# Recurrent attention and gated MLP layer on eight cores: fp32 transposes of the normalised input, an earlier place for the row-sum reciprocals, shorter wait lists in the down projection and at the fences

## The chip, the cores and the metric

One Trainium2 chip, eight cores, the same program on each, every core with two of the sixteen sequences; nothing passes between cores. The metric is device time in microseconds (us) of the slowest core. The engines are named as the profile names them: PE (matmuls), PEld (its weight loads), DVE (vector), ACT (scalar), POOL and SP. SP issues most DMAs; ACT's queue also issues some.

## The reference, cut to what matters

```python
xn = _layernorm(x)                         # x: 16 x 2048 x 1024, fp32
q, k, v = split_heads(xn @ Wq + bq), ...   # 16 heads of 64
att = softmax(causal(q @ k.T / 8))
y   = (att @ v) @ Wo + bo
s   = (y - mu) * rsqrt(var + eps) * gamma + beta
h   = silu(xn @ wg.T / 127) * (xn @ wu.T / 127)     # 3072 hidden, int weights
g   = silu(h @ wd.T / 127)
x   = x + s * g
```

## The kernel before, in words

Precision is kept by splitting fp32 values in two bf16 parts, "hi" (the rounded value) and "lo" (the rest), and multiplying hi by hi, hi by lo and lo by hi. All instructions are listed in program order for each engine (`W.op`), with the tokens each one waits for; an engine runs its list strictly in that order. Every compute engine has one counting semaphore (`c_te`, `c_ve`, `c_se`, `c_ge`), and a token is a value of it.

The stages, one after another with a fence between (`W.fence`, line 109: each engine puts a nop that waits for the DMAs it has issued, and everything behind the fence waits for the nops of all engines):

1. Once: weights are split or transposed and written to DRAM (lines 240 to 335).
2. For each of the two sequences, LayerNorm. A first pass reads 16 tiles of 128 tokens for the sums (lines 358 to 388). The second pass (lines 390 to 434) reads each tile again; ACT writes the normalised tile once as bf16 (`hi`, line 397) and once as fp32 (`v6`, line 402); DVE subtracts them (`lo`, line 409); PE transposes the eight 128x128 blocks of hi, and then those of lo, through one PSUM bank in bf16 (line 420), and DVE copies the bank into the arena after each eight (line 427). The bank is used again only after that copy.
3. Attention for eight head pairs (`hg`). Per pair: K and Q projections (line 551), V projection (line 603) with fp32 transposes of V (line 623), and then four query blocks (`qb`) of 512 columns. Block `qb` has `4 qb + 4` key chunks `sc`. The order of issue for each chunk is: scores of `sc` for two heads (line 736, on the diagonal also a mask matmul, line 745), exponentials of `sc` on ACT (line 760), then attention times V of chunk `sc - 1` (line 783, fp32) into banks 3 and 4, whose row 64 collects the row sums.
   The end of a block is `emit_evac` (line 660). It is called for block `qb` when scores and exponentials of chunk 0 of block `qb + 1` have been issued, and for the last block straight behind it. For each of the two heads: ACT takes Ln (line 667) and Exp with scale -1 (line 671) of the row sums, a one-row matmul spreads the reciprocals over 128 partitions into bank 5 (line 675), ACT copies bank 5 out (line 679), and DVE multiplies (line 684). The second head's matmul waits for the first head's copy, because both use bank 5. Then come the hi and lo parts (lines 694, 699) and two DMAs from ACT's queue, the second of which waits for lo.
4. Output projection (line 897) and the second LayerNorm.
5. Gated MLP for eight blocks of 256 tokens. For each of 24 hidden chunks `hc`: gate matmuls (line 1017), up matmuls (line 1029), and the chain Silu on ACT (line 1039), product on DVE (line 1045), hi on ACT (line 1054), lo on DVE (line 1059). Gate and up use banks 0 to 3 by parity. Then the down projection (line 1093) over the same 24 chunks into the same banks 0 to 3, weights coming through two buffers of two chunks each, refilled from SP's queue.

Of the kernel before, what the change touches and what calls it, by code (L numbers as in the profile page):

```python
# [57 lines left out]
class W:  # L58
    def __init__(self, nc, ctx):
        self.nc = nc  # L60
        self.ctx = ctx
        self.ops = {e: [] for e in ENG}
        self.nsem = 0
        self.barrier = []
        self.fence_sem = self.sem("fence")
        self.qsem = {e: self.sem("q_" + e) for e in ("sync", "scalar", "gpsimd")}
        self.dma_sems = {e: [self.qsem[e]] for e in ("sync", "scalar", "gpsimd")}
        self.phase_ops = {e: 0 for e in ENG}
# [38 lines left out]
    def fence(self):  # L107
        toks = []
        for e in ENG:
# [35 lines left out]
def build_program():  # L145
# [79 lines left out]
    c_ge = w.sem("c_ge")  # L225

# [109 lines left out]
    for b in range(B_PER_CORE):  # L336
# [8 lines left out]
        hi_tm = [PB[:, 16384:17408], PB[:, 17408:18432]]  # L345
        lo_tm = [PB[:, 18432:19456], PB[:, 19456:20480]]
# [3 lines left out]
        hl_cons = [[], []]  # L350
# [39 lines left out]
        for tt in range(16):  # L390
# [5 lines left out]
            hi = w.op("scalar", (lambda e, d=hi_tm[s], x_=xt[s], tt=tt:  # L396
                                 e.activation(d[:, :], x_[:, :], AF.Identity,
                                              bias=rb16[:, tt:tt + 1],
                                              scale=r16[:, tt:tt + 1])),
                      waits=[tok, s3] + hl_cons[s], inc=c_se)  # L400
# [4 lines left out]
                      waits=[tok] + xn_cons[s], inc=c_se)  # L405
            xt_cons[s] = [v6, hi]
            xn_cons[s] = []
            lo = w.op("vector", (lambda e, d=lo_tm[s], a=xnt[s], h=hi_tm[s]:
                                 e.tensor_sub(d[:, :], a[:, :], h[:, :])),
                      waits=[hi, v6] + hl_cons[s], inc=c_ve)  # L410
            xn_cons[s] = [lo]
            hl_cons[s] = []
            for part, src_t in ((0, hi_tm[s]), (1, lo_tm[s])):
                bank = pbt2[0]
                tk = None
                for dc in range(8):
                    tk = w.op("tensor",
                              (lambda e, a=bank[:, dc * 128:(dc + 1) * 128],
                               b=src_t[:, dc * 128:(dc + 1) * 128]:
                               e.transpose(a, b, idb_s[:, :])),  # L420
                              waits=[hi if part == 0 else lo] + pbtc[0],
                              inc=c_te)
                hl_cons[s].append(tk)
                base = part * 8
                ev = w.op("vector",
                          (lambda e, tt=tt, base=base, bank=bank:
                           e.tensor_copy(
                               AA[:, :].rearrange(
                                   "p (dc t) -> p dc t", dc=16)
                               [:, base:base + 8, tt * 128:(tt + 1) * 128],  # L430
                               bank[:, 0:1024].rearrange("p (dc j) -> p dc j",
                                                         dc=8))),
                          waits=[tk], inc=c_ve)
                pbtc[0] = [ev]
                aa_done.setdefault(tt // 4, []).append(ev)
# [48 lines left out]
        for hg in range(8):  # L484
# [175 lines left out]
            def emit_evac(av_l, sh, qb_e):  # L660
                mul_toks = []
                for hh in range(2):
                    bank = pb[3 + hh]
                    lrow = vfm[0:1, 1024 + hh * 512:1024 + hh * 512 + 512]
                    rc0 = w.op("scalar",
                               (lambda e, d=lrow, s_=bank:
# [524 lines left out]
```

How the kernel before makes its waits and increments, by code:

```python
                def runner(eng, e=e):  # L126
                    mark = {}
                    for fn, waits, inc, n in self.ops[e]:
                        for sem, v in waits:
                            k = id(sem)
                            if mark.get(k, 0) >= v:
                                continue
                            eng.wait_ge(sem.h, v)
                            mark[k] = v
                        ins = fn(eng)
                        if inc is not None:
                            ins.then_inc(inc.h, n)
```

## Time and profile before

| | |
|---|---|
| median of the runs shown | 7750.89 us (7289.63, 7750.89, 8067.74) |
| the profiled execution | 7289.63 us |
| its span, slowest core (core 4) | 7288.1 us; all cores 7240.3 to 7288.1 |
| PE busy | 5710.1 us, 78% of the span |
| ACT busy, DVE busy | 1670.6 us, 1365.5 us |
| mean granted clock of PE, by core | 0.918 to 0.923 |

A row of the timeline reads: start in us from the span's start, time in us until the end of the last of them, engine, line, operation, written<-read, shapes, count; in brackets, the engine's idle time before it and what it was put down to. A row of the table by stretch reads: stretch, its length, then busy time with the number of instructions for PE, PEld, DVE, ACT and POOL, then the granted clock of PE (1.00 is 2.4 GHz, 0.50 is 1.2 GHz), the DMA engines' busy share and GB/s. A row of the table by line reads: instructions and their count, busy us and mean ns of one, idle us of the engine before them and what ended it. A modelled matmul duration contains its latency, so overlapping matmuls can add up to more than their run takes.

### The profile page before, as it was taken

How to read it: one execution, taken by the hardware profiler on the slowest of the kernel's cores; microseconds unless marked ns; L12 is line 12 of the kernel's file. 1: busy time of each engine (PE TensorE's matmuls, PEld its weight loads, DVE VectorE, ACT ScalarE, POOL GpSimd, SP SyncE). 2: the span in 40 equal slices, each digit the busy share in tenths (PEclk: the TensorE clock that was granted, in tenths of full speed). 3: DMA queues.
4: the chain of work that ended last, by engine and by line, in shares of the span. 5: the costliest groups of instructions: out<-in, count | busy, mean ns of one | idle time of the engine just before them, and what ended most of it. 6: DMA issues, size and time to landing. Idle time of an engine off the chain costs nothing.

```text
span 7288.1 us, 79655 instructions; the slowest of 8 cores (7240.3 to 7288.1 us)
## 1 busy us (share of the span) xinstructions
PE 5710.1 (78%) x30120; PEld 2859.5 (39%) x30328; DVE 1365.5 (19%) x2326; ACT 1670.6 (23%) x3020; POOL 130.5 (2%) x124
## 2 busy tenths in 40 slices
PE   0113888888888895999895788888888885989998
PEld 0112333322333244676573332233322333766765
DVE  0013111101111014111122311111111214111111
ACT  0003322333223301111112223322233211111111
POOL 5000000000000000000000000000000000000000
PEclk9999988988889897999997798889988887999999
DMA  7454000000000033666665100000000032666666
GB/s 206 75 90 123 14 13 14 11 9 14 13 12 6 27 95 84 156 153 149 153 157 146 42 13 6 13 13 14 13 6 13 6 88 62 150 146 156 153 146 145
DMA packets 1510254, 529.74 MB, mean 73 GB/s; under 512 B 1383670, under 2 KB 1474038, under 8 KB 1509884
## 3 DMA queue, kind: packets, MB, share of 16 engines
q1 hardware_dynamic: 1394940, 436.53, 25.6%
q10 hardware_dynamic: 106880, 69.22, 3.1%
q0 software_dynamic: 8064, 18.88, 1.9%
q8 instruction: 253, 4.15, 0.3%
q14 instruction: 117, 0.96, 0.1%
HBM read 474.19 MB, written 69.21 MB: 75 GB/s over the span
## 4 chain that ended last, share of the span: by engine, by line
PE 72%; DMA 13%; DVE 5%; ACT 4%; issue 3%; SPq 1%; POOL 1%; DVEq 0%; ACTq 0%; POOLq 0%
PE pb L783 15%; PE pb L551 9%; PE pb L736 9%; PE pb L1029 9%; PE pb L1017 9%; DMA pool_b<-scr_wblk 6%; PE pb L1093 5%; PE pb L603 5%; PE pb L897 5%; DMA scr_wblk<-pool_b 4%; PE pb L675 3%; PE pb L745 1%; SPq L104 1%; ACT pool_f L671 1%; ACT pool_f L667 1%
## 5 line engine op out<-in xcount | busy, mean ns | idle before, releaser
L783 PE MATMUL pb<-pool_f 128*65 128x512 f32 (+3 forms) x2560 | 1147.6, 578 | 0.0
L760 ACT ACTIVATE pool_f<-pb,tiny 128x512 f32<-128x512 f32 (+3 forms) x1280 | 755.1, 621 | 1539.4 <-PE pb L745 1003.4
L1017 PE MATMUL pb<-arena_a,pool_b 128*128 128x256 bf16 x6144 | 738.0, 274 | 176.7 <-DMA pool_b<-scr_wblk 175.1
L1093 PE MATMUL pb<-pool_b 128*128 128x512 bf16 x3008 | 691.1, 383 | 145.8 <-DMA pool_b<-scr_wblk 122.3
L1029 PE MATMUL pb<-arena_a,pool_b 128*128 128x256 bf16 x6144 | 734.5, 273 | 14.5 <-ACT pool_f L1105 11.3
L551 PE MATMUL pb<-arena_a,pool_b 128*128 128x512 bf16 x3008 | 694.8, 390 | 32.1 <-DMA pool_b<-scr_whilo 19.8
L1017 PEld LDWEIGHTS pb<-arena_a,pool_b 128*128 128x128 bf16 x6144 | 601.2, 98 | 258.2 <-issue 186.3
L736 PE MATMUL pb<-pool_b 64*128 64x512 bf16 (+3 forms) x3840 | 698.6, 382 | 0.5 <-ACT pool_f L760 0.4
L1029 PEld LDWEIGHTS pb<-arena_a,pool_b 128*128 128x128 bf16 x6144 | 600.0, 98 | 90.3 <-issue 20.3
L783 PEld LDWEIGHTS pb<-pool_f 128*65 128x65 f32 x2560 | 324.9, 147 | 515.4 <-issue 495.4
L1093 PEld LDWEIGHTS pb<-pool_b 128*128 128x128 bf16 x3072 | 292.8, 98 | 540.7 <-issue 221.0
L684 DVE TENSOR_TENSOR pool_f<-pb,pool_f 64x512 f32<-64x512 f32 x128 | 87.5, 683 | 2176.3 <-ACT pool_f L679 2176.3
L551 PEld LDWEIGHTS pb<-arena_a,pool_b 128*128 128x128 bf16 x3072 | 298.6, 100 | 420.6 <-issue 101.7
L736 PEld LDWEIGHTS pb<-pool_b 64*128 64x128 bf16 x3840 | 200.5, 98 | 630.4 <-issue 548.2
L675 PE MATMUL pb<-pool_f,tri_s 1*128 1x512 f32 x256 | 213.3, 925 | 298.1 <-ACT pool_f L671 298.1
L291 PE MATMUL pbt<-idb_s,pool_b 128*128 128x128 bf16 x384 | 48.5, 306 | 435.8 <-DMA scr_wblk<-pool_b 281.6
L603 PE MATMUL pb<-arena_a,pool_b 128*128 128x512 bf16 x1488 | 365.1, 402 | 5.5 <-issue 3.9
L897 PE MATMUL pb<-pool_b 128*128 128x512 bf16 x1504 | 338.7, 386 | 30.7 <-DMA pool_b<-scr_o 29.1
L1054 ACT ACTIVATE pool_b<-pool_f 128x256 bf16<-128x256 f32 x384 | 159.9, 416 | 723.7 <-DVE pool_f L1045 723.7
L1045 DVE SCALAR_TENSOR_TENSOR pool_f<-pb,pool_f 128x256 f32<-128x256 f32 x384 | 163.1, 425 | 760.4 <-PE pb L1017 694.5
L897 PEld LDWEIGHTS pb<-pool_b 128*128 128x128 bf16 x1536 | 152.1, 99 | 219.4 <-issue 44.1
L603 PEld LDWEIGHTS pb<-arena_a,pool_b 128*128 128x128 bf16 x1536 | 156.2, 103 | 194.2 <-issue 44.4
(82 smaller groups left out, 2640.3 us busy)
## 6 DMA issues: line engine op xcount, KB each, us to landing
pool_b<-scr_wblk SPq DMA_DIRECT2D x1152, 256.0 KB, 3.5
pool_f<-x SPq DMA_DIRECT2D x96, 512.0 KB, 4.3
pool_b<-scr_o SPq DMA_DIRECT2D x64, 512.0 KB, 5.3
pool_b<-scr_whilo SPq DMA_DIRECT2D x96, 256.0 KB, 4.0
scr_whilo<-pool_b ACTq DMA_DIRECT2D x64, 256.0 KB, 4.7
scr_o<-pool_b ACTq DMA_DIRECT2D x128, 128.0 KB, 1.8
y<-pool_f ACTq DMA_DIRECT2D x32, 512.0 KB, 3.9
scr_wblk<-pool_b ACTq DMA_DIRECT2D x48, 256.0 KB, 4.9
```

Of the source, the lines that this page charges most:

```text
L551: e.matmul(o, l, r, start=st, stop=sp)),
L603: e.matmul(o, l, r, start=st, stop=sp)),
L675: e.matmul(pb[5][:, 0:512], tri_s[0:1, 0:128], d, start=True, stop=True)),
L736: e.matmul(o, l, r, start=st, stop=sp, tile_position=tp)),
L760: e.activation(d, s_, AF.Exp, bias=bc)),
L783: e.matmul(o, l, r, start=st, stop=sp)),
L897: e.matmul(o, l, r, start=st, stop=sp)),
L1017: e.matmul(o, l, r, start=st, stop=sp)),
L1029: e.matmul(o, l, r, start=st, stop=sp)),
L1045: e.scalar_tensor_tensor(d[:, :], s_[:, 0:256], 1.0 / 127.0, a[:, :], AL.mult, AL.mult)),
L1054: e.activation(d, a[:, :], AF.Copy)),
L1093: e.matmul(o, l, r, start=st, stop=sp)),
```

## The change

It has four parts.

- The fence's nop of an engine now also waits for that engine's own compute semaphore.
- LayerNorm, second pass: ACT writes the normalised tile once, as fp32. PE transposes its eight blocks in fp32, four to a bank, taking the six fp32 banks in turn. From each bank ACT copies the bf16 hi part to the arena and DVE subtracts the hi part from the bank and writes lo to the arena. The bf16 transposes, the two DVE copies and the ACT pass for hi are gone.
- Attention: Ln and Exp of both heads' row sums are issued at the end of their own query block, directly behind the last attention-times-V matmuls, and no longer in `emit_evac`, which takes over their tokens.
- Down projection: the first matmuls of the four banks waited for the hi and lo parts of all 24 chunks; they now wait for those of chunk 0. The matmuls of later chunks wait for their own chunk, as before.

```diff
@@ W.fence
+            cs = self.csem.get(e)
+            if cs is not None and cs.count:
+                w.append(Tok(cs, cs.count, e, True))
@@ build_program
+    w.csem = {"vector": c_ve, "scalar": c_se, "tensor": c_te, "gpsimd": c_ge}
@@ LayerNorm, second pass, for tt in range(16)
-            hi = w.op("scalar", ... activation(hi_tm[s], xt[s], AF.Identity, bias, scale),
-                      waits=[tok, s3] + hl_cons[s], inc=c_se)
             v6 = w.op("scalar", ... activation(xnt[s], xt[s], AF.Identity, bias, scale),
-                      waits=[tok] + xn_cons[s], inc=c_se)
+                      waits=[tok, s3] + xn_cons[s], inc=c_se)
-            lo = w.op("vector", ... tensor_sub(lo_tm[s], xnt[s], hi_tm[s]),
-                      waits=[hi, v6] + hl_cons[s], inc=c_ve)
-            for part, src_t in ((0, hi_tm[s]), (1, lo_tm[s])):
-                bank = pbt2[0]
-                for dc in range(8):
-                    tk = w.op("tensor", ... transpose(a, b, idb_s[:, :]),
-                              waits=[hi if part == 0 else lo] + pbtc[0], inc=c_te)
-                ev = w.op("vector", ... tensor_copy(AA[...], bank[:, 0:1024]), waits=[tk])
-                pbtc[0] = [ev]
+            for g2_ in range(2):
+                bank = pb[(tt * 2 + g2_) % 6]
+                tks = []
+                for j in range(4):
+                    dc = g2_ * 4 + j
+                    tks.append(w.op("tensor", ... transpose(o, xnt[s][dc], idf_s[:, :]),
+                                    waits=[v6] + pbk_cons[(tt * 2 + g2_) % 6], inc=c_te))
+                xn_cons[s].append(tks[-1])
+                hi = w.op("scalar", ... activation(aa3[hi part], bank[:, 0:512], AF.Copy),
+                          waits=[tks[-1]], inc=c_se)
+                lo = w.op("vector", ... tensor_sub(aa3[lo part], bank[:, 0:512], aa3[hi part]),
+                          waits=[tks[-1], hi], inc=c_ve)
+                pbk_cons[(tt * 2 + g2_) % 6] = [hi, lo]
@@ attention
-            def emit_evac(av_l, sh, qb_e):
+            def emit_evac(av_l, sh, qb_e, rcs):
...
-                    rc0 = w.op("scalar", ... activation(lrow, bank[64:65, 0:512], AF.Ln),
-                               waits=[av_l[hh]] + lrow_cons[hh], inc=c_se)
-                    rc = w.op("scalar", ... activation(lrow, lrow, AF.Exp, scale=-1.0),
-                              waits=[rc0], inc=c_se)
+                    rc = rcs[hh]
...
                 emit_av(prev)
-                evac_pend[0] = (dict(av_last), qb % 2, qb)
+                rcs = {}
+                for hh in range(2):
+                    lrow = vfm[0:1, 1024 + hh * 512:1024 + hh * 512 + 512]
+                    rc0 = w.op("scalar", ... activation(lrow, pb[3 + hh][64:65, 0:512], AF.Ln),
+                               waits=[av_last[hh]] + lrow_cons[hh], inc=c_se)
+                    rcs[hh] = w.op("scalar", ... activation(lrow, lrow, AF.Exp, scale=-1.0),
+                                   waits=[rc0], inc=c_se)
+                evac_pend[0] = (dict(av_last), qb % 2, qb, rcs)
@@ down projection
-                                       waits=([t3] + hi_toks + pbk_cons[tt2 * 2 + oh])
+                                       waits=([t3, hi_toks[0], hi_toks[1]]
+                                              + pbk_cons[tt2 * 2 + oh])
                                        if (hc == 0 and xs == "h") else [...],
```

## Rows read from the trace of the kernel before

**Rows 1.** The page, part 1: busy time by engine.
```profile
PE 5710.1 (78%) x30120; PEld 2859.5 (39%) x30328; DVE 1365.5 (19%) x2326; ACT 1670.6 (23%) x3020; POOL 130.5 (2%) x124
```
**Rows 2.** Busy time by stretch: attention, gated MLP (first sequence); LayerNorm second pass (second).
```profile
705.00:2531.00 1826.00, 1582.32 (x6107) 550.88 (x6160) 299.20 (x537) 586.14 (x991) 0.00 (x0) 0.89 0.05 12
2811.00:3933.00 1122.00, 1022.77 (x7646) 747.14 (x7676) 202.10 (x416) 171.66 (x417) 0.00 (x0) 0.99 0.65 150
...
3983.00:4048.00 65.00, 32.35 (x256) 24.75 (x256) 39.93 (x49) 38.06 (x33) 0.00 (x0) 0.50 0.37 115
```
**Rows 3.** Timeline, PE and ACT, from one query block to the next.
```profile
839.40 1.47 PE L783 MATMUL pb<-pool_f 128*65 128x256 f32 x8
...
840.80 0.83 PE L736 MATMUL pb<-pool_b 64*128 64x512 bf16 x6
841.72 1.27 ACT L760 ACTIVATE pool_f<-pb,tiny 128x512 f32<-128x512 f32 x2 [1.69 <-PE pb L736]
843.01 0.59 ACT L667 ACTIVATE pool_f<-pb 1x512 f32<-1x512 f32 x1
843.69 0.63 ACT L671 ACTIVATE pool_f<-pool_f 1x512 f32<-1x512 f32 x1
...
844.46 1.09 PE L675 MATMUL pb<-pool_f,tri_s 1*128 1x512 f32 x2 [2.83 <-ACT pool_f L671]
845.65 0.59 ACT L679 COPY pool_f<-pb 128x512 f32<-128x512 f32 x1 [1.33 <-PE pb L675]
...
847.71 2.04 PE L675 MATMUL pb<-pool_f,tri_s 1*128 1x512 f32 x2 [2.16 <-ACT pool_f L671]
...
849.68 1.47 PE L736 MATMUL pb<-pool_b 64*128 64x512 bf16 x6
...
851.08 2.99 PE L783 MATMUL pb<-pool_f 128*65 128x512 f32 x4
...
853.30 1.27 ACT L760 ACTIVATE pool_f<-pb,tiny 128x512 f32<-128x512 f32 x2 [1.30 <-PE pb L783]
...
857.49 1.93 PE L783 MATMUL pb<-pool_f 128*65 128x512 f32 x4
```
**Rows 4.** Timeline, PE and ACT, behind the last block of a head pair.
```profile
5867.49 1.47 PE L783 MATMUL pb<-pool_f 128*65 128x256 f32 x8
5868.83 0.59 ACT L667 ACTIVATE pool_f<-pb 1x512 f32<-1x512 f32 x1 [0.72 <-PE pb L783]
...
5870.28 1.09 PE L675 MATMUL pb<-pool_f,tri_s 1*128 1x512 f32 x2 [1.33 <-ACT pool_f L671]
...
5873.53 1.33 PE L675 MATMUL pb<-pool_f,tri_s 1*128 1x512 f32 x2 [2.16 <-ACT pool_f L671]
```
**Rows 5.** By line, whole span: the row-sum matmuls, four records for each block end.
```profile
L675 PE MATMUL pb<-pool_f,tri_s 1*128 1x512 f32 x256 | 213.3, 925 | 298.1 <-ACT pool_f L671 298.1
```
**Rows 6.** Busy time in one stretch behind the first row-sum matmul.
```profile
846.40:853.20 6.80, 5.49 (x11) 1.55 (x12) 2.06 (x3) 2.29 (x4) 0.00 (x0) 0.50 0.04 14
```
**Rows 7.** Timeline: four fp32 transposes of V, then LayerNorm's second pass.
```profile
775.37 0.63 PE L623 MATMUL pb<-idf_s,pool_f 128*128 128x128 f32 x4 [1.01 <-DVE pool_f L613]
...
3983.58 1.24 ACT L397 ACTIVATE pool_b<-pool_f 128x1024 bf16<-128x1024 f32 x1 [0.37 <-DVE pool_f L388]
...
3985.07 1.01 PE L420 MATMUL pbt<-idb_s,pool_b 128*128 128x128 bf16 x8 [61.40 <-ACT pool_b L397]
...
3993.05 1.24 ACT L397 ACTIVATE pool_b<-pool_f 128x1024 bf16<-128x1024 f32 x1 [1.01 <-PE pbt L420]
...
3996.97 1.24 ACT L397 ACTIVATE pool_b<-pool_f 128x1024 bf16<-128x1024 f32 x1 [1.54 <-PE pbt L420]
```
**Rows 8.** Timeline: start of a down projection; and, by line, its matmuls.
```profile
2895.53 1.91 PE L1029 MATMUL pb<-arena_a,pool_b 128*128 128x256 bf16 x16
...
2899.44 1.89 PE L1093 MATMUL pb<-pool_b 128*128 128x512 bf16 x8 [2.00 <-DMA pool_b<-scr_wblk]
...
L1093 PE MATMUL pb<-pool_b 128*128 128x512 bf16 x3008 | 691.1, 383 | 145.8 <-DMA pool_b<-scr_wblk 122.3 <-DVE pool_b L1059 20.0
```

More of the change, by code:

```diff
@@ L349, in build_program @@
         xn_cons = [[], []]
-        hl_cons = [[], []]
         sq_cons = []
@@ new lines, in build_program @@
+            for g2_ in range(2):
[3 more added lines that the diff above has]
+                    dc = g2_ * 4 + j
+                    tks.append(w.op("tensor",
+                                    (lambda e, o=bank[:, j * 128:(j + 1) * 128],
+                                     s_=xnt[s][:, dc * 128:(dc + 1) * 128]:
+                                     e.transpose(o, s_, idf_s[:, :])),
+                                    waits=[v6] + pbk_cons[(tt * 2 + g2_) % 6],
+                                    inc=c_te))
+                xn_cons[s].append(tks[-1])
+                pbk_cons[(tt * 2 + g2_) % 6] = []
+                aa3 = AA[:, :].rearrange("p (dc t) -> p dc t", dc=16)
+                hi = w.op("scalar",
+                          (lambda e, tt=tt, g2_=g2_, bank=bank,
+                           d=aa3[:, g2_ * 4:g2_ * 4 + 4, tt * 128:(tt + 1) * 128]:
+                           e.activation(d,
+                                        bank[:, 0:512].rearrange(
+                                            "p (dc j) -> p dc j", dc=4),
+                                        AF.Copy)),
+                          waits=[tks[-1]], inc=c_se)
+                lo = w.op("vector",
+                          (lambda e, tt=tt, g2_=g2_, bank=bank,
+                           d=aa3[:, 8 + g2_ * 4:8 + g2_ * 4 + 4,
+                                 tt * 128:(tt + 1) * 128],
+                           h=aa3[:, g2_ * 4:g2_ * 4 + 4, tt * 128:(tt + 1) * 128]:
+                           e.tensor_sub(d,
+                                        bank[:, 0:512].rearrange(
+                                            "p (dc j) -> p dc j", dc=4), h)),
+                          waits=[tks[-1], hi], inc=c_ve)
+                pbk_cons[(tt * 2 + g2_) % 6] = [hi, lo]
+                aa_done.setdefault(tt // 4, []).append(lo)
@@ L664, in emit_evac @@
                     lrow = vfm[0:1, 1024 + hh * 512:1024 + hh * 512 + 512]
-                    rc0 = w.op("scalar",
-                               (lambda e, d=lrow, s_=bank:
-                                e.activation(d, s_[64:65, 0:512], AF.Ln)),
-                               waits=[av_l[hh]] + lrow_cons[hh], inc=c_se)
-                    rc = w.op("scalar",
-                              (lambda e, d=lrow:
-                               e.activation(d, d, AF.Exp, scale=-1.0)),
-                              waits=[rc0], inc=c_se)
+                    rc = rcs[hh]
                     bm = w.op("tensor",
```

38 lines of the change are left out of this document (8 added, 30 removed).

## Prediction

> **What bounds the kernel now.** I read the page's busy times first: PE is busy 5710.1 of 7288.1 us, the next engine, ACT, 1670.6 [rows 1]. Then the busy times by stretch, to see where PE's idle time lies. An attention stage takes 1826 us with 1582 of PE, so some 244 us idle twice, at a mean granted clock of 0.89; the MLP takes 1122 with 1023 of PE, at 0.99; the second LayerNorm pass takes about 64 us with 32 of PE, at 0.50 [rows 2]. So PE's order sets the end, and a gain is worth what it takes from PE's idle time or gives back in clock. The timeline of one block boundary shows the largest repeated hole. Scores of the next block run from 840.80 to 841.63, and the next scores start at 849.68: 8.05 us with only two row-sum matmuls in them [rows 3]. There are 2 x 8 x 4 = 64 block ends, 48 with a next block of their head pair and 16 without. The row by line gives all of them: 298.1 idle and 213.3 busy, (298.1 + 213.3) / 64 = 7.99 us for one [rows 5].
>
> **The hole, step by step.** In ACT's list stand the two exponentials of the new block (841.72 to 842.99), Ln, Exp (to 844.32), the wait for the first matmul (844.46 to 845.55), the copy (845.65 to 846.24), then the second Ln and Exp, and only then the second matmul at 847.71. The first Exp ends 0.14 before its matmul starts [rows 3]. The clock falls too: it is 0.50 from 846.4 to 853.2 [rows 6], so the second matmul takes 2.04 and not 1.09, the six score matmuls 1.47 and not 0.83, the four records of line 783 2.99 and not 1.93 [rows 3]. That is 0.95 in the hole and 0.64 + 1.06 = 1.70 behind it.
>
> **Reciprocals issued earlier, 48 inner boundaries.** The run of line 783 ends at 840.87 [rows 3]. Behind a last block Ln starts 0.13 before that end (5868.83 against 5867.49 + 1.47), and the matmul 1.45 after Ln [rows 4]. So the new order gives: Ln at 840.74, Exp at 841.42 to 842.05, first matmul 842.19 to 843.28; second Ln 842.07, second Exp 842.75 to 843.38; the new block's exponentials only then, 843.40 to 844.67 (they started at 841.72, so 1.68 later); the copy 844.69 to 845.28; the second matmul, whose reciprocals are long there, at 845.42. It was 847.71: 2.29 earlier at the same speed. What waits behind the added ACT work is the exponentials and, behind them, the copy; PE can't use the exponentials before the second matmul is through, since that stands before the next scores in its list.
> If the second matmul also runs at full clock, 0.95 more. The boundary shown is one of the shorter ones: mean matmul time is 213.3 / 64 = 3.33 against 3.13 here, and a slow first matmul is now covered, as it has until 844.69. I take 2.7 for the hole and 0.6 of the 1.70 behind it, since a shorter hole should be followed by a shorter slow stretch, but 3.8 us in front of the second matmul still hold only 1.1 of PE work, so I expect the clock to fall again. 3.3 x 48 = 158 us.
> Bounds: below, 2.29 x 48 = 110, nothing from the clock. Above, the exponentials of the second chunk: they start 5.59 after the second matmul (853.30 less 847.71), 0.95 less at full clock, so at 850.06, 3.24 earlier than now; with about 0.7 of slack there today, 3.9 x 48 = 187.
>
> **16 last blocks.** No exponentials stand in between. Ln and Exp of the second head end at about 5871.47 beside the first matmul (5870.28 to 5871.37), the copy ends at 5872.08, and the second matmul starts at 5872.22, not 5873.53 [rows 4]: 1.31 earlier, or 2.26 with full clock. I take 1.7: 27 us; bounds 21 and 36.
>
> **Down projection, 16 starts.** The up matmuls end at 2897.44 and the first down matmul waits until 2899.44, 2.00 us [rows 8], the length of the chain Silu, product, hi and lo of chunk 23 that its list asks for. The timeline's row puts this wait down to a DMA; but SP issues those weights behind the up weights of chunk 23, which go out when chunk 21's up matmuls end, and the row by line names lo (line 1059) for 20.0 us, ten starts of 2.00 [rows 8]. I take all 16 as this wait. With the new list bank 0 waits for Silu of chunk 22, bank 1 for Silu of chunk 23 (its gate ended an up phase, 1.9 us, earlier), bank 3 for the product of chunk 23, six matmuls of 0.22 later; chunk 23's lo is 23 chunks away. The weight refills are set off by the matmuls that free a buffer, so they move up as well. 16 x 2.00 = 32 us; bounds 0 (the loads don't come earlier) and 32.
>
> **LayerNorm, 32 tiles.** Now a tile takes 3.92 (3993.05 to 3996.97), set by the single bank: two rounds of transposes and copy [rows 7]. The new order is serial on ACT: fp32 pass 1.23, 0.25 to PE (3983.58 + 1.24 to 3985.07), four fp32 transposes, hi copy, the second hi copy, and only then the next tile, since both copies stand ahead of it in ACT's list. A 512-column copy takes 0.59 (line 679) [rows 3]. Four fp32 transposes take 0.63 at full clock, 0.12 apart [rows 7], and DVE or ACT start 0.10 later. Full clock: 1.23 + 0.25 + 0.73 + 0.59 + 0.59 = 3.39, 17 us less in 32 tiles. But this stage runs at 0.50 [rows 2]. With steps of 0.24: first set 0.27 + 0.72 + 0.10 = 1.1, second set 0.96 behind it, copy 0.59: 4.15, so 0.25 x 32 = 8 us more. I take the 8, the clock of the stage's own row; 17 less is the other end. DVE's two subtractions and the banks are off this chain.
> The row shows the clock at 0.50 through a stage in which PE transposes half of the time. The Trainium skill, "TensorE: Matmul & The Clock Gate", Part 4: PE-mode transpose, says that the full clock doesn't engage for transposes; by that rule the loss of 8 holds for the new order too, without it the gain of 17 would be open. The trace agrees, by that 0.50.
>
> **Fences.** Six nops wait for their own engine's last instruction, at most the 0.14 of one hand-over: 1 us. With the old order no work is hidden there, so it is all cost.
>
> **Sum.** 158 + 27 + 32 - 8 - 1 = 208 us. The profiled execution took 7289.63 (span 7288.1 and 1.5 around it): 7082. The median shown, 7750.9, stands 461 above that execution; the forecast is for one like the profiled, which has the lowest time shown. The same saving would be 2.7% of the median and is 2.9% of the profiled time.
>
> **Rivals.**
> Only the queues get shorter. The clock falls as long as before and refills are no earlier: 110 + 21 - 8 - 1 = 122, 7168 us. For it: the clock fell in each boundary I looked at, and a hole stays. Against it: at least ten starts wait 2.00 for a chain that is gone [rows 8].
> The clock comes back sooner, and LayerNorm's transposes run at full speed: 187 + 36 + 32 + 17 - 1 = 271, 7019 us. For it: the second matmul and the work behind it lose 2.65 us at each boundary now. Against it: the 0.50 of rows 2.
> Slower: PE runs at 1.2 GHz for longer after each of the 64 block ends, because the work now comes back in two short pieces and not in one. Each us of such a stretch costs 0.5 us of work. To be 2% (146 us) slower it has to undo 208 us too: 354 / 64 = 5.5 us of work each, 11 us more of slow stretch behind a stretch that is now 6.8 [rows 6]. 7436 us. Against it: the hole gets shorter in every reading of rows 3.
>
> **How the numbers follow.** Forecast 0.67, only the queues 0.13, sooner clock 0.17, slower 0.03. A measurement can tell about 2%, 146 us, from no change, so the point is 7144. The forecast and the sooner clock lie below it: faster 0.84. Only the queues is within 2%: 0.13. Slower 0.03. The forecast's own range is 7040 to 7130. The range goes from 7000, a little below the sooner clock's 7019, to 7180, a little above the 7168 of the queues alone; only the slow case and what I have not thought of are outside.
>
> **What would show each step.** In the timeline of a boundary: Ln directly behind the last line-783 matmul and before the exponentials; the second row-sum matmul 3.8 us after the scores instead of 6.1; the by-line idle time of that matmul down from 298 to about 150, with a total for its idle and busy time near 5.3 x 64 = 340. Attention stages about 93 us shorter each. The start of the down projection: no idle time, MLP stages 16 us shorter each. LayerNorm tiles 4.1 us apart. The prediction is wrong if the down projection's buffers wait 2 us longer at chunk 4, if the slow stretches behind a boundary don't shrink, or if PE now waits for the exponentials of the second chunk.

## The result, and the profile after

| | before | changed |
|---|---|---|
| profiled execution, us | 7289.63 | 7120.75 |
| its slowest core, us | 7288.1 | 7119.2 |
| median of the eight cores' spans in it, us | 7277.2 | 7091.4 |
| median of all runs, us (lowest to highest) | 7854.13 (7289.63 to 8101.77; 14 runs) | 7373.59 (7102.66 to 7768.13; 13 runs) |

The ratio of the changed kernel to the one before is 0.974, with a 95% interval of 0.968 to 0.980. In some executions of either kernel the cores of one die are granted a lower clock for part of the time; the medians of all runs contain these executions, the ratio and all comparisons below leave them out.

So the change makes the kernel 2.6% faster. The forecast of 7082 was a ratio of 7082 / 7289.63 = 0.9715, inside the interval; the profiled execution took 39 us more than forecast and lies in the range; the median of all runs, 7373.59, lies outside it, above 7180.

The page of the changed kernel, part 1, beside [rows 1]: busy time by engine.

```profile
span 7119.2 us, 79579 instructions; the slowest of 8 cores (7074.6 to 7119.2 us)
...
PE 5716.5 (80%) x30072; PEld 2859.4 (40%) x30072; DVE 1329.2 (19%) x2294; ACT 1661.2 (23%) x3052; POOL 130.0 (2%) x124
```

PE is as busy as before, 5716.5 against 5710.1 us, in a span that is 169 us shorter. The page shows core 5. All lines of the changed kernel below are of core 4, the core that the page of before shows; its span is 7091.6.

The busy times by stretch answer to [rows 2]: attention and gated MLP of the first sequence, LayerNorm's second pass of the second. Columns: stretch, its length, busy us (and instructions) of PE, PEld, DVE, ACT and POOL, granted clock, share of DMA, GB/s.

```profile
704.00:2459.00 1755.00, 1578.78 (x6120) 551.65 (x6176) 302.53 (x541) 584.49 (x998) 0.00 (x0) 0.90 0.05 12
2740.00:3842.00 1102.00, 1021.30 (x7647) 746.63 (x7677) 199.60 (x414) 170.59 (x415) 0.00 (x0) 0.99 0.66 152
...
3917.00:3978.00 61.00, 24.74 (x102) 19.43 (x102) 17.89 (x27) 28.68 (x38) 0.00 (x0) 0.50 0.45 118
```

The attention stretch went from 1826 to 1755 us with 1582 and 1579 of PE: its idle time fell from 244 to 176 us. The MLP stretch is 20 us shorter. The transposes of LayerNorm still run at 0.50.

The stage times that I use from here on are the median over the eight cores, from the first to the last record of the lines that make up a stage. Two numbers are the first and the second sequence.

| stage | before | changed | difference | forecast |
|---|---|---|---|---|
| attention with K, Q, V | 1809.3, 1808.9 | 1728.8, 1729.0 | -80.4, -79.9 | -92.5 each |
| gated MLP | 1111.6, 1106.4 | 1098.6, 1090.2 | -13.0, -16.2 | -16 each |
| LayerNorm's second pass, and the way from it to K | 72.5, 72.2 | 73.5, 73.0 | +1.0, +0.8 | +4.5 each, with the fences |
| first stage (work that the change leaves alone) | 601.6 | 607.7 | +6.1 | 0 |
| the rest | | | about -4 | 0 |
| span | 7277.2 | 7091.4 | -185.8 | -208 |

The first stage alone took 588.9 to 607.7 us in the profiled executions of five kernels (before, changed, p_evac, p_down, a_fill) that all have it unchanged, and the two MLP stages 1085.0 to 1098.6 and 1084.4 to 1090.2 in two runs of the changed kernel. Differences of some 10 us in one stage of two runs are therefore not evidence of anything. The rows of single waits are.

The timeline of one block boundary answers to [rows 3]: PE and ACT, start, length, engine, line and operation, and in brackets the idle time before it and what ended it.

```profile
844.74 1.47 PE L778 MATMUL pb<-pool_f 128*65 128x256 f32 x8
846.08 0.59 ACT L804 ACTIVATE pool_f<-pb 1x512 f32<-1x512 f32 x1 [0.72 <-PE pb L778]
846.13 0.83 PE L731 MATMUL pb<-pool_b 64*128 64x512 bf16 x6
846.76 0.63 ACT L808 ACTIVATE pool_f<-pool_f 1x512 f32<-1x512 f32 x1
847.30 0.57 ACT L804 ACTIVATE pool_f<-pb 1x512 f32<-1x512 f32 x1
847.53 1.09 PE L670 MATMUL pb<-pool_f,tri_s 1*128 1x512 f32 x2 [0.57 <-ACT pool_f L808]
...
848.62 1.27 ACT L755 ACTIVATE pool_f<-pb,tiny 128x512 f32<-128x512 f32 x2
849.77 0.59 ACT L674 COPY pool_f<-pb 128x512 f32<-128x512 f32 x1
850.50 2.02 PE L670 MATMUL pb<-pool_f,tri_s 1*128 1x512 f32 x2 [1.88 <-ACT pool_f L674]
...
852.45 1.47 PE L731 MATMUL pb<-pool_b 64*128 64x512 bf16 x6
853.85 3.66 PE L778 MATMUL pb<-pool_f 128*65 128x512 f32 x4
...
856.06 1.27 ACT L755 ACTIVATE pool_f<-pb,tiny 128x512 f32<-128x512 f32 x2 [1.30 <-PE pb L778]
```

Ln starts at 846.08, before the last attention-times-V matmul has ended, and both Ln and Exp pairs are through before the new block's exponentials at 848.62. The second row-sum matmul waits for the copy and no longer for an Exp. The hole between two groups of scores is 852.45 - 846.96 = 5.49 us, where [rows 3] showed 8.05. The clock still falls in this one: the second row-sum matmul takes 2.02 us and the scores behind it 1.47. Where exactly it falls differs from boundary to boundary: over the 48 on core 4 the second row-sum matmul took 1.09 us (full clock) in 14 and 1.54 in the mean, where before it took 2.04 in all 48. The row of the stretch behind the hole shown answers to [rows 6].

```profile
850.60:857.40 6.80, 6.80 (x12) 1.40 (x12) 1.99 (x3) 2.48 (x4) 0.00 (x0) 0.50 0.11 39
```

By line, whole span, beside [rows 5] and the second row of [rows 8]: the row-sum matmuls and the down projection. Columns: count, busy us, mean ns, idle before it and by what it was ended.

```profile
L670 PE MATMUL pb<-pool_f,tri_s 1*128 1x512 f32 x256 | 175.7, 771 | 152.4 <-ACT pool_f L674 101.8 <-ACT pool_f L808 50.7
...
L1099 PE MATMUL pb<-pool_b 128*128 128x512 bf16 x3008 | 681.4, 380 | 112.0 <-DMA pool_b<-scr_wblk 106.1 <-DVE pool_f L1051 1.5 <-issue 0.6
```

A block end now costs (152.4 + 175.7) / 64 = 5.13 us, where it cost 7.99. The idle time before the down matmuls fell by 33.8 us, and most of the wait for the lo part is gone from the row (20.0 us before, 1.5 of DVE now). The start of a down projection, PE and DVE, shows it once, beside the first rows of [rows 8]:

```profile
2825.17 1.91 PE L1035 MATMUL pb<-arena_a,pool_b 128*128 128x256 bf16 x16
2827.23 6.85 PE L1099 MATMUL pb<-pool_b 128*128 128x512 bf16 x31
2828.29 0.43 DVE L1065 TENSOR_TENSOR pool_b<-pool_f,pool_b 128x256 bf16<-128x256 f32 x1 [0.61 <-ACT pool_b L1060]
2834.84 0.38 PE L1099 MATMUL pb<-pool_b 128*128 128x512 bf16 x1 [0.76 <-DMA pool_b<-scr_wblk]
```

The down matmuls start 0.15 us behind the up matmuls, and the product of the last chunk is formed beside them. Over the 16 starts of core 4 this gap sums to 3.1 us; before it was 32.0.

LayerNorm's second pass, beside the second part of [rows 7]:

```profile
671.72 1.23 ACT L399 ACTIVATE pool_f<-pool_f 128x1024 f32<-128x1024 f32 x1
673.20 1.94 PE L413 MATMUL pb<-idf_s,pool_f 128*128 128x128 f32 x8 [2.07 <-ACT pool_f L399]
674.38 0.60 ACT L422 ACTIVATE arena_a<-pb 128x512 bf16<-128x512 f32 x1 [1.43 <-PE pb L413]
675.23 0.60 ACT L422 ACTIVATE arena_a<-pb 128x512 bf16<-128x512 f32 x1 [0.26 <-PE pb L413]
675.73 1.23 ACT L399 ACTIVATE pool_f<-pool_f 128x1024 f32<-128x1024 f32 x1
```

A tile takes 675.73 - 671.72 = 4.01 us, serial on ACT as forecast, with the eight transposes at 1.2 GHz.

### The profile page after: what moved, and what is told of

Its sections match the earlier page's. It is cut to its first block, busy times and chain, and to the rows that moved or that the text cites. A ratio compares the mean times of both kernels' runs of the same rounds, so it can differ in the third digit from the quotient of the medians.

```text
span 7119.2 us, 79579 instructions; the slowest of 8 cores (7074.6 to 7119.2 us)
## 1 busy us (share of the span) xinstructions
PE 5716.5 (80%) x30072; PEld 2859.4 (40%) x30072; DVE 1329.2 (19%) x2294; ACT 1661.2 (23%) x3052; POOL 130.0 (2%) x124
## 4 chain that ended last, share of the span: by engine, by line
PE 73%; DMA 13%; DVE 4%; ACT 4%; issue 4%; SPq 1%; POOL 1%; ACTq 0%; DVEq 0%; POOLq 0%
PE pb L778 15%; PE pb L553 10%; PE pb L1035 9%; PE pb L1023 9%; PE pb L731 8%; DMA pool_b<-scr_wblk 6%; PE pb L1099 5%; PE pb L605 5%; PE pb L903 5%; DMA scr_wblk<-pool_b 4%; PE pb L670 2%; PE pb L740 1%; DMA scr_whilo<-pool_b 1%; SPq L105 1%; DMA pool_f<-x 1%
## 5 line engine op out<-in xcount | busy, mean ns | idle before, releaser
L553 PE MATMUL pb<-arena_a,pool_b 128*128 128x512 bf16 x3072 | 713.9, 392 | 21.9 <-DMA pool_b<-scr_whilo 21.9
L605 PE MATMUL pb<-arena_a,pool_b 128*128 128x512 bf16 x1536 | 372.2, 403 | 0.0
L670 PE MATMUL pb<-pool_f,tri_s 1*128 1x512 f32 x256 | 182.0, 797 | 152.8 <-ACT pool_f L674 102.0
```

What stands on the lines that cost most here:

```text
L553: e.matmul(o, l, r, start=st, stop=sp)),
L605: e.matmul(o, l, r, start=st, stop=sp)),
L670: e.matmul(pb[5][:, 0:512], tri_s[0:1, 0:128], d, start=True, stop=True)),
```

## Experiments

Eleven kernels ran. after_again is the changed kernel once more; p_ are parts of the change made alone on the kernel before; b_ is an addition to the kernel before; a_ are additions to the changed kernel. "Boundary" below is the mean over the 48 block ends with a next block of their head pair (core 4), counted from the end of the new block's first scores.

### The attention part alone: p_evac

```diff
@@ kernel before: only the attention part of the change
-            def emit_evac(av_l, sh, qb_e):
+            def emit_evac(av_l, sh, qb_e, rcs):
-                    rc0 = w.op("scalar", ... AF.Ln ...)
-                    rc = w.op("scalar", ... AF.Exp ...)
+                    rc = rcs[hh]      # issued behind the block's last AV matmuls
```

> The kernel before with only the attention part of the change: Ln and Exp of the row sums at the end of their own block. Theory (the hole behind a query block is set by the order of ACT's list): the two attention stages get about 80 us shorter each, as in the changed kernel (1809 to 1729 us from the first projection to the last row-sum matmul), all other stages keep their times; in all 160 us less than before, ratio 0.978. The second row-sum matmul starts 3.5 us behind the scores, not 6.1 to 7.3. Rival (the attention stages gain from what the fences or the LayerNorm part leave behind, the phase in which PE's clock is entered for one): less than 120 us.

Measured: 7120.87 us lowest, ratio 0.979 [0.976, 0.982]. The attention stages take 1736.3 and 1735.3, that is 73.0 and 73.6 us less than before. By line, the row-sum matmuls of p_evac:

```profile
L668 PE MATMUL pb<-pool_f,tri_s 1*128 1x512 f32 x256 | 186.5, 815 | 152.7 <-ACT pool_f L672 101.3 <-ACT pool_f L806 51.4
```

Idle 152.7 against 298.1 in [rows 5], and nearly the 152.4 of the whole change. This one part carries 147 of the 186 us (160 was expected). The kernel p_ln_fence below, which ran on the same chip and has the old order, takes 148 us more in its attention stages, so the part does not need the others.

### The down projection's waits alone: p_down

```diff
@@ kernel before, first down matmul of each bank
-                                       waits=([t3] + hi_toks + pbk_cons[tt2 * 2 + oh])
+                                       waits=([t3, hi_toks[0], hi_toks[1]]
+                                              + pbk_cons[tt2 * 2 + oh])
```

> The kernel before with only the shorter wait lists of the down projection. Theory: the 2.00 us in front of each of the 16 down projections go, nothing gives them back; 29 to 32 us less, ratio 0.996, the MLP stages 15 us shorter each. Rival (the refills of the two weight buffers set the pace of the down projection, so PE meets a longer wait at chunk 4): the idle time moves behind chunk 3, MLP stages less than 5 us shorter each.

Measured: 7256.02 us lowest. Its MLP stages take 1089.8 and 1081.7. The two kernels that ran on the same chip with it and have the old waits took 1101.7 and 1097.8 (p_evac), 1101.8 and 1098.6 (p_ln_fence): 12 and 16.5 less, 28.5 in both. By line, the down matmuls of p_down:

```profile
L1093 PE MATMUL pb<-pool_b 128*128 128x512 bf16 x3072 | 685.7, 379 | 92.7 <-DMA pool_b<-scr_wblk 91.8 <-issue 0.2
```

The idle time is 92.7, and what is left of it is ended by weight DMAs. The 145.8 of [rows 8] is not its fair neighbour: that row has 3008 records, so 64 matmuls are missing from the trace and their time may count as idle. p_evac and p_ln_fence, with all 3072 records, show 128.6 and 129.1, some 36 more than p_down. That the loads move up with the matmuls is borne out: behind the first down matmul of each block the idle time sums to 92 us, where those two kernels have 100, and the longest single wait is 2.35 us against 2.95 and 2.73.

### LayerNorm and the fences: p_ln_fence

```diff
@@ kernel before, W.fence and LayerNorm's second pass, as in the change (the last lines in words)
+            cs = self.csem.get(e)
+            if cs is not None and cs.count:
+                w.append(Tok(cs, cs.count, e, True))
...
-            hi, v6 (ACT), lo (DVE); bf16 transposes into pbt2[0], 2 copies (DVE)
+            v6 (ACT); 8 fp32 transposes into two of pb[0..5]; 2 hi copies (ACT), 2 lo (DVE)
```

> The kernel before with only the LayerNorm part and the waits at the fences, which it needs, since it uses banks that the next stage writes. Theory (serial chain on ACT, fp32 transposes 0.24 us apart because PE stays at 1.2 GHz in this stage): a tile every 4.01 us instead of 3.92, the tail of the stage 1 us longer, in all 2 to 5 us more than before, no difference that the ratio can show. Rival (the LayerNorm part is what gains): 15 us less or more.

Measured: 7272.16 us lowest, ratio 1.0015 [0.9992, 1.0039]. The second pass takes 0.7 us less in each sequence and the way from it to K 1.3 and 1.5 more. This part changes nothing that can be measured. The fence waits alone were not run.

The three parts sum to -147 - 28.5 + 1.5 = -174; the whole change shows -186. Stages that the change leaves alone wander by 6 to 10 us, so no interaction of the parts can be told from this.

### What the clock costs: a_fill and b_fill

a_fill puts matmuls that nothing reads into the holes before the row-sum matmuls, into an fp32 bank in the place of the unused bf16 one. It tells PE's missing clock from PE's missing work: the row sums have to wait as long as before, but PE is not idle.

```diff
@@ changed kernel, emit_evac, ahead of each row-sum matmul
+                    for fi in range(2 if hh == 0 else 8):
+                        w.op("tensor", (lambda e: e.matmul(pb6[:, 0:512], idb_s[:, :],
+                                        QHI[:, 0:512], start=True, stop=True)), inc=c_te)
```

> The changed kernel with added PE work in the hole: two idle 512-column bf16 matmuls in front of the first row-sum matmul and eight in front of the second, into a bank that nothing reads. Theory (PE's fall to 1.2 GHz behind each block end still costs what it did): the granted clock stays at 1.00 through the boundary, scores of the second chunk start 4.6 us behind those of the first instead of 5.0, scores of the fourth 11.7 instead of 12.5; 0.8 x 48 and about 1 x 16 us, so 45 to 60 us less than the changed kernel, although PE has more work. Rival (ACT's chain of copy, product, hi, lo and DMA in front of the second chunk's exponentials is what bounds the boundary now, the slow clock lies beside it): less than 15 us less, or some us more.

Measured: 6987.92 us lowest, ratio 0.9645 [0.958, 0.971] to the kernel before. The attention stages take 1688.0 and 1688.8, that is 41 and 40 us less than in the changed kernel; I had expected 45 to 60 for both together. PE in a boundary of a_fill:

```profile
829.33 0.83 PE L738 MATMUL pb<-pool_b 64*128 64x512 bf16 x6
830.09 0.60 PE L671 MATMUL pb<-pool_b,idb_s 128*128 128x512 bf16 x2
830.73 1.09 PE L677 MATMUL pb<-pool_f,tri_s 1*128 1x512 f32 x2
831.76 1.90 PE L671 MATMUL pb<-pool_b,idb_s 128*128 128x512 bf16 x8
833.70 1.09 PE L677 MATMUL pb<-pool_f,tri_s 1*128 1x512 f32 x2
834.72 0.83 PE L738 MATMUL pb<-pool_b 64*128 64x512 bf16 x6
835.48 2.02 PE L785 MATMUL pb<-pool_f 128*65 128x512 f32 x4
```

The order and the waits are those of the changed kernel, but the second row-sum matmul takes 1.09 and the scores 0.83: PE stays at 2.4 GHz. The stretch of this hole:

```profile
829.50:836.00 6.50, 6.42 (x28) 1.92 (x24) 1.06 (x2) 4.43 (x8) 0.00 (x0) 1.00 0.00 0
```

On core 4 the clock is full through all 48 boundaries, from the first scores to the fourth chunk's. So the fall follows from what PE does in the hole: idle time and two pairs of one-row matmuls, which this run doesn't tell apart. In a boundary the fourth chunk's scores come at 11.76 us, 0.73 earlier than the changed kernel's 12.49, which is 35 us in 48. From the first K matmul to the first V matmul it takes 49.54 us and not 51.45, mean over the 16 head pairs (14 of them follow a last block), another 31. From the first scores of a head pair to the end of its second block's first scores it takes 14.47 us and not 16.24, another 28. These are the figures of core 4, whose attention stages are 98 us shorter in sum; the median core's are 81. What I had left out of my expectation are the projections and the first block: slow stretches lie over them too. The total is 117 us less than the changed kernel's; some 35 of that lie in the first stage and the MLPs, which have no such matmuls. I don't claim them.

b_fill does the same in the kernel before, with 12 and 9 matmuls for its longer holes; LayerNorm's bf16 transposes go to the other bf16 bank, which frees the space.

> The kernel before, order unchanged, with idle 512-column bf16 matmuls in the hole of each block end: twelve in front of the first row-sum matmul, nine in front of the second, into a bank that nothing reads. Tells how much of the change's gain a full clock alone would have brought. Theory (order and clock are two separate costs of the hole): clock 1.00 through the boundary; the second row-sum matmul stays 6.1 us behind the scores, the next scores start 7.1 us behind them instead of 8.4, scores of the fourth chunk about 14 instead of 16; behind the 16 last blocks the twelve matmuls are 1.3 us longer than the wait they fill, against 2 to 3 us of faster projections. 48 x 1.9 + 16 x 1.2 = 110 us less than before, ratio about 0.985. Rival (the gain of the change was clock only): ratio near 0.976 here too.

Measured: 7173.94 us lowest, ratio 0.9835 [0.979, 0.988]; attention stages 1766.7 and 1768.9, 83 us less than before in both. By line:

```profile
L682 PE MATMUL pb<-pool_f,tri_s 1*128 1x512 f32 x256 | 140.2, 626 | 16.3 <-ACT pool_f L672 5.4
```

All row sums run at 2.4 GHz, and yet the next scores come at 7.17 us: the hole is what ACT's order makes it. Before, they came at 8.40; with the change at 5.01; with the change and the matmuls at 4.58. Order and clock are two separate costs here: the order gives 160 us in the attention stages with the clock falling and 159 with it held ((1766.7 + 1768.9) - (1688.0 + 1688.8) = 158.8); the added matmuls give 83 in the old order and 81 in the new. That is net of their own time, and even with them the clock is not full everywhere: the first block of a head pair takes 14.5 and 14.7 us in the mean, where the shortest take 13.6.

### A second bank for the row sums: a_twobank, a_twobank_late

In the changed kernel the second row-sum matmul waits for the copy of the first, as both use one bank, and the copy stands behind the exponentials. a_twobank gives each head its own bank and its own place for the copy.

```diff
@@ changed kernel, emit_evac
+                    bb = pb[5] if hh == 0 else pb6
+                    lv = vfm[:, hh * 512:hh * 512 + 512]
-                               waits=[rc] + pbk_cons[5], inc=c_te)
+                               waits=[rc] + (pbk_cons[5] if hh == 0 else pb6_cons[0]), inc=c_te)
```

> The changed kernel with the second head's row-sum matmul into a bank of its own and its copy into a region of its own, so that it waits for its reciprocals alone. Theory (what holds it at 3.5 us is the first head's copy, behind the delayed exponentials): it starts 1.7 us behind the scores, the next scores at 2.8; but the exponentials of the second chunk stand behind copies, products, hi, lo and a DMA, at about 7 us, so scores of the third chunk wait for them and the fourth's start at 10 to 10.5, not 12.5: 2 to 2.5 us in each of 48 and about 1 in each of 16, 110 to 135 us less than the changed kernel. Rival (ACT's chain already bounds): less than 60 us less.

Measured: 6965.12 us lowest; attention stages 1665.9 and 1665.2, 127 us less than the changed kernel in both. A boundary, PE and ACT:

```profile
825.43 2.15 PE L675 MATMUL pb<-pool_f,tri_s 1*128 1x512 f32 x4 [0.72 <-ACT pool_f L817]
827.51 0.83 PE L740 MATMUL pb<-pool_b 64*128 64x512 bf16 x6
829.03 3.58 PE L787 MATMUL pb<-pool_f 128*65 128x512 f32 x4 [0.70 <-DVE pool_f L688]
...
831.64 1.26 ACT L764 ACTIVATE pool_f<-pb,tiny 128x512 f32<-128x512 f32 x2 [1.31 <-DVE pool_b L703]
```

Both row sums run in one piece and the next scores come 2.87 us behind the first, where the changed kernel needs 5.01. Two waits are next: PE's attention-times-V waits for DVE's product (0.70), and ACT's exponentials of the second chunk come only behind the lo part on DVE, since the output's DMAs, which wait for lo, stand ahead of them in ACT's list. a_twobank_late issues hi, lo and both DMAs one chunk later, behind those exponentials.

```diff
@@ a_twobank, emit_evac keeps (mul_toks, sh, qb_e); block loop:
+                    if sc == 1 and evac_late[0] is not None:
+                        emit_late(*evac_late[0])     # hi, lo and the two DMAs
+                        evac_late[0] = None
```

> As the kernel with two banks, and hi, lo and the two DMAs of a block issued behind the exponentials of the next block's second chunk. Theory: those exponentials start at about 4 us instead of 7, nothing waits for them, scores of the fourth chunk start about 9 us behind those of the first; 1.2 us less in each of 48 boundaries than with two banks alone, so 50 to 70 us. Rival (PE's clock or the products bound by then): less than 20 us less than with two banks alone.

Measured: 6910.94 us lowest, ratio 0.948 [0.943, 0.953]; attention stages 1646.3 and 1639.2, 46 us less again. The boundary of this kernel:

```profile
820.28 1.30 ACT L768 ACTIVATE pool_f<-pb,tiny 128x512 f32<-128x512 f32 x2
820.86 3.52 PE L791 MATMUL pb<-pool_f 128*65 128x512 f32 x4 [0.70 <-DVE pool_f L689]
824.31 0.83 PE L744 MATMUL pb<-pool_b 64*128 64x512 bf16 x6
```

ACT doesn't wait for lo any more: the exponentials of the second chunk come at 3.97 us where they came at 7.09. The wait for the product stays, and the fourth chunk's scores come at 9.69 us, not at the 9 that I had expected; (10.66 - 9.69) x 48 is 47 us, and so it is 46 and not the 50 to 70 expected.

### LayerNorm with one tile ahead: a_lnpipe

```diff
@@ changed kernel, LayerNorm's second pass
+        v6p = ln_head(0)
+        for tt in range(16):
+            v6n = ln_head(tt + 1) if tt < 15 else None    # load and fp32 pass of the next tile
+            ln_tail(tt, v6p)                              # transposes, hi, lo
+            v6p = v6n
```

> The changed kernel with the fp32 pass of LayerNorm's next tile issued in front of the two hi copies of this one, so that ACT works while PE transposes. Theory (4.01 us a tile is the serial chain on ACT): a tile takes the 2.75 us that the loads of x take with two buffers, 32 x 1.2 = 35 to 40 us less than the changed kernel, everything else the same. Rival (the transposes at 1.2 GHz or the subtractions on DVE bound): a tile takes over 3.5 us, less than 16 us less.

Measured: 7058.74 us lowest; the second pass takes 42.8 and 43.4 us (cores 4 to 7) and not 61.6 twice, 37 in both. Two places of its timeline on core 6, and the stretch around them:

```profile
3880.29 1.07 PE L417 MATMUL pb<-idf_s,pool_f 128*128 128x128 f32 x8 [0.92 <-ACT pool_f L399]
...
3884.71 1.24 ACT L399 ACTIVATE pool_f<-pool_f 128x1024 f32<-128x1024 f32 x1 [0.67 <-DMA pool_f<-x]
...
3887.59 1.24 ACT L399 ACTIVATE pool_f<-pool_f 128x1024 f32<-128x1024 f32 x1 [0.67 <-DMA pool_f<-x]
...
3870.00:3900.00 30.00, 19.13 (x84) 15.60 (x84) 13.43 (x22) 22.24 (x31) 0.00 (x0) 0.56 0.60 183
```

A tile takes 3887.59 - 3884.71 = 2.88 us where 2.75 was expected, now set by ACT and the load of x behind it. The stage is bound by the serial chain that the prediction described; with the chain broken it gives what the change by itself does not.

### All together: after_again, a_best, a_best_fill

after_again is the changed kernel once more, beside the two last ones on their chip. a_best is a_twobank_late with a_lnpipe's order; a_best_fill adds matmuls that nothing reads in what is left of the holes: two (five behind a last block) ahead of the first row sum, and three ahead of the first attention-times-V matmuls.

> The changed kernel once more, beside the two combined ones. Expected as in its own result: ratio 0.974 to the kernel before, attention stages near 1729 us each.

> The changed kernel with all three edits: two banks for the row-sum matmuls, hi, lo and DMAs behind the second chunk's exponentials, and LayerNorm's next fp32 pass issued first. Theory (the gains are in separate stages and add up): attention stages 1643 us each as with the first two, LayerNorm's second pass 43 us as with the third, 6855 us, ratio 0.941 to the kernel before. Rival (denser work gives some back, in clock or in the loads): above 6880.

> The same with idle 512-column bf16 matmuls where PE still waits at a block end: two (five behind a last block) in front of the first row-sum matmul, three in front of the new block's first attention-times-V. Theory (the slow clock behind a hole still costs, 2.5 us of slow stretch within 14 us of an inner boundary, 6.8 behind a last block): clock mostly 1.00, 1 us less in each of 48 and 2 us in each of 16, 50 to 80 us less than without them, near 6790 us. Rival (the idle matmuls take what they bring): within 20 us of the kernel without them.

Measured: after_again 7091.97 us lowest, median core span 7075.6; a_best 6872.43 and 6867.1 (the median of cores 0 to 3 alone); a_best_fill 6866.11 and 6852.0. The kernel before took 7262.1 at its lowest on this chip, so a_best stands at 6872.43 / 7262.1 = 0.946 of it; that is a ratio of two lowest times, without an interval. Against after_again a_best gives 209 us more, as the sum of its parts (127 + 46 + 37 = 210) says; it lies between the expected 6855 and the rival's 6880. The added matmuls then give no more than 15, where I had expected 50 to 80. In an inner boundary the fourth chunk's scores come at 9.92 us with them and at 9.69 without. They don't hold the clock there; scores behind the hole and the stretch around them, core 0 of a_best_fill:

```profile
829.83 1.47 PE L760 MATMUL pb<-pool_b 64*128 64x512 bf16 x6
...
829.00:836.00 7.00, 7.00 (x17) 1.54 (x16) 2.06 (x3) 3.35 (x7) 0.00 (x0) 0.51 0.11 37
```

PE is busy through all of this stretch and still at 0.51. So this run does not show whether the clock has nothing left to give there or whether two and three matmuls are too few to hold it. Where they gain is behind the last blocks: there the row sums run at full clock (second pair 1.09 us and not 2.04) and the next K comes at 3.56 and not 4.90.

## Why the prediction was right, and where it failed

**The range failed at its centring.** The step is "The median shown, 7750.9, stands 461 above that execution; the forecast is for one like the profiled". The working and the range of 7000 to 7180 are for an execution like the profiled one, and that of the changed kernel took 7120.75, the lowest 7102.66. The median of its 13 runs is 7373.59: nine of them lie above 7180. The three times shown for the kernel before had that spread, 7289.63 to 8067.74; a range for the median had to reach over it. The effect itself was forecast as 0.9715 and measured as 0.974.

**The hole, inner boundaries: the sum right, one of its two terms wrong.** Forecast 3.3 us each, 2.7 in the hole and 0.6 behind it, and the second row-sum matmul 3.79 us behind the scores. Measured from the end of the new block's first scores to the scores of the fourth chunk: 15.98 before, 12.49 after, 3.49 us, and the matmul at 3.54 where it came at 6.43. By line it is 298.1 to 152.4 idle, where about 150 was said, and 328 us idle and busy, where 340 was said. But the split is another. The hole, up to the second chunk's scores, went from 8.40 to 5.01, 3.39 us: 2.89 by the order (the boundary of [rows 3] was one of the shorter ones, 6.08 against a mean of 6.43) and 0.50 by the second matmul's clock. From the second to the fourth chunk's scores it is 7.58 before and 7.48 after. So "a shorter hole should be followed by a shorter slow stretch" failed: of the 0.6 it was to bring, 0.10 came. The time at low clock fell from 4.60 to 1.11 us within the hole, and behind it, up to the fourth chunk's scores, only from 4.50 to 4.22; on core 1 it rose there, from 3.86 to 4.10. That the sum fits is a larger gain in the hole in the place of one behind it, which is luck. The prediction named slow stretches that don't shrink as a sign of being wrong; behind the hole they didn't.

**The 16 last blocks: the start right, the clock wrong.** Forecast 27 us, 1.7 each: 1.31 for the earlier start and some 0.4 for the clock. The timeline behind a last block, beside [rows 4]:

```profile
5700.70 1.47 PE L778 MATMUL pb<-pool_f 128*65 128x256 f32 x8
...
5703.50 1.27 PE L670 MATMUL pb<-pool_f,tri_s 1*128 1x512 f32 x2 [1.33 <-ACT pool_f L808]
5705.59 2.04 PE L670 MATMUL pb<-pool_f,tri_s 1*128 1x512 f32 x2 [0.82 <-ACT pool_f L674]
```

The second matmul starts 5705.59 - 5700.70 = 4.89 us behind the last V matmuls' start, where [rows 4] gives 6.04: 1.15 earlier. In the mean of the 16 it starts 1.30 earlier, as forecast, but it takes 1.98 us where it took 1.97: the clock gives nothing. (The one shown in [rows 4] takes 1.33, so the 0.95 that the prediction adds for its full clock could not be had from that row.) K starts 1.27 us sooner, mean of the 14 blocks that a K projection follows, and from K to V it then takes 51.45 where it took 50.99, 0.46 more. 16 x (1.27 - 0.46) = 13 us, half of the term. This is a mis-sized term; the lower bound of 21 was above it, as it had no price for what follows in the projections. With matmuls in the holes K to V takes 49.54 in the new order (a_fill) and 49.50 in the old (b_fill): the slow stretch cost the projections 1.5 us before the change and 1.9 after it.

**The rest of the attention stages.** The inner term makes 3.49 x 48 = 168 and the outer 13, 181 in sum, but the stages got 160 shorter. Per head pair on core 4 the blocks' body went from 139.99 to 130.37 us, 9.62 less, where three boundaries make 10.5. The missing 0.85 us per head pair, 14 us in all, lie in the first block, from a head pair's first scores to the end of the second block's first scores: 15.40 us before and 16.24 after in the mean. PE has no idle time in it, only its clock differs. Two such stretches of before and one of after:

```profile
1248.45:1262.04 13.59, 13.59 (x55) 4.76 (x54) 0.16 (x1) 4.22 (x8) 0.00 (x0) 0.75 0.03 5
1474.24:1490.92 16.68, 16.68 (x55) 5.29 (x54) 0.16 (x1) 4.22 (x8) 0.00 (x0) 0.59 0.02 3
...
1239.25:1255.85 16.60, 16.60 (x55) 5.29 (x54) 0.16 (x1) 5.01 (x10) 0.00 (x0) 0.59 0.03 6
```

The same 55 matmuls take 13.6 us at a granted clock of 0.75 or 16.6 at 0.59. Before, 8 of the 16 first blocks were of the long kind (3 lay between), after it 14. All eight cores have a longer mean than before. The prediction had no term for it, and no run shows why the low clock lies over more of them; with matmuls in the holes (a_fill) the mean is 14.47. Some 7 us more lie between core 4 and the median core.

**Down projection: right.** Forecast 32, and all 16 starts as one wait. The gap summed to 32.0 us before and to 3.1 after, and p_down gave 28.5.

**LayerNorm and fences: right in mechanism, 4.15 against 4.01 us a tile.** Forecast +9 with the fences; measured about +2. The 0.14 us by which a tile is shorter than forecast is 4 us over 32 tiles; the terms listed there add up to 4.13, not 4.15. The second end, 17 us less at full clock, did not come: the row shows 0.50. The Trainium skill, "TensorE: Matmul & The Clock Gate", Part 4, says that the full clock doesn't engage for transposes; in this kernel the trace agrees, in a_lnpipe it does not hold (last section).

**The rivals.** "Only the queues get shorter" (7168) is out as a whole: the down projection's wait is gone, and the second row-sum matmul takes 0.50 us less. On the work behind the hole it was nearer than the forecast, which is the 0.10 above. "The clock comes back sooner" (7019) is out: the work behind the hole gained 0.10 and not 1.70, and LayerNorm's transposes stayed at 0.50. a_fill, with PE busy in the hole, takes 81 us more from the attention stages. "Slower" is out: the first blocks did get slower, but by 14 us in all, and the low clock from a boundary's first to its fourth scores fell from 9.1 to 5.3 us.

## What to carry to other kernels

In the list of an in-order engine, put the short operations on which another engine's next instruction hangs ahead of long ones that nobody waits for yet: here four one-row operations ahead of two exponentials were 147 us of 186, and a bank of its own and a later place for two DMAs in the same list were worth 173 more. Price a hole on PE twice, by its idle time and by what runs at 1.2 GHz behind it, in the next stage too; the two were separate costs here (160 and 81 us), and unread matmuls in the hole show the second one apart. A shorter hole did not shorten the slow stretch behind it. Where the executions shown spread over hundreds of us, a range worked out from one of them holds for its like and not for a median over all.

## What the runs showed of the hardware that I had not expected

One-row fp32 matmuls in a hole do not keep the clock. In the changed kernel the first row-sum matmul takes 1.09 us and the second, 1.88 us of idle time later, 2.02; the granted clock of the stretch behind is 0.50. With 2 and 8 unread matmuls over 128 rows in the same places it stays at 1.00. Whether the one-row shape matters beyond the idle time beside it, no run here separates.

A stretch with nothing on PE but fp32 transposes can run above 0.50. In a_lnpipe eight transposes took 1.07 us in one tile (2.4 GHz) and 1.94 in another (1.2 GHz), and the granted clock of that 30 us stretch is 0.56; in the changed kernel, with the same transposes further apart, it is 0.50. By what the Trainium skill, "TensorE: Matmul & The Clock Gate", Part 4, says of transposes it would be 0.50 in both; here the measurement decides.

One and the same stretch of matmuls without any idle time takes 13.6 or 16.6 us, at a granted clock of 0.75 or 0.59, within one execution (the first blocks above).

The time of stages that no kernel changed moves with the run: the first stage took 588.9 to 607.7 us in the five profiled executions compared. No run here shows why.
